# Flamingo-style gated cross-attention with a quantised FFN: projections, y and denominators of two segments in one cluster

## The reference, cut to what matters

```python
def _L0_xattn_ref(latents, context, ...):       # latents: layernorm(x), 2048 x 256; context: 1601 x 256
    lat = layernorm(latents, ln_l_w, ln_l_b)
    ctx = layernorm(context, ln_c_w, ln_c_b)
    q = (lat @ Wq).reshape(b, n, H, D).transpose(0, 2, 1, 3)      # H = 16 heads, D = 64
    k, v = jnp.split(ctx @ Wkv, 2, axis=-1)                       # heads as q
    attn = jnp.einsum('bhnd,bhsd->bhns', q, k) * D ** (-0.5)
    attn = jax.nn.softmax(jnp.clip(attn, -11.0, 11.0), axis=-1)
    out = jnp.einsum('bhns,bhsd->bhnd', attn, v)
    return out.transpose(0, 2, 1, 3).reshape(b, n, INNER) @ Wo + bo
x = x + jnp.tanh(g_xattn[0]) * _L0_xattn_ref(_layernorm(x, axis=-1), ctx_1024, ...)
x = x + jnp.tanh(g_ffn[0]) * _L0_ffn_ref(_layernorm(x, axis=-1), w_gate, w_up, w_down)
```

## Time and profile before

| | before |
|---|---|
| median of 3 runs | 1151.55 us (1150.32 to 1151.62) |
| the profiled execution | 1151.44 us, span 1149.6 us |
| PE busy | 1075.3 us, 94% of the span |
| DVE busy | 1006.2 us, 88% |
| ACT busy | 604.5 us, 53% |
| chain that ended last | PE 80%, DVE 9%, ACT 5%, issue 5% |
| granted TensorE clock, mean | 0.981 |

### The profile page before, as it was taken

One profiled execution on the slowest core, in us unless ns is written; L12 is line 12 of the kernel. 1 busy time (PEld: TensorE's weight loads), 2 busy tenths in 40 slices (PEclk: granted clock), 3 DMA queues, 4 the chain that ended last, 5 costly groups with the idle time before them and its releaser, 6 DMA issues.

```text
span 1149.6 us, 20469 instructions
## 1 busy us (share of the span) xinstructions
PE 1075.3 (94%) x8342; PEld 501.4 (44%) x8342; DVE 1006.2 (88%) x1390; ACT 604.5 (53%) x706; POOL 37.0 (3%) x41
## 2 busy tenths in 40 slices
PE   5999999999999999999999999999999998999059
PEld 3443344434443444344434443444344323887049
DVE  7687988898989898999898989887999999749996
ACT  3555555555555555555555555554555464449652
POOL 0500000000000000000000000000000000003200
PEclk9999999999999999999999999999999999999579
DMA  8001300010001000100010001000000000000002
GB/s 264 18 20 25 120 20 20 20 38 20 20 20 37 20 20 20 38 20 19 21 38 20 20 20 38 20 20 20 30 20 19 20 29 10 1 1 1 0 0 74
DMA packets 37860, 34.57 MB, mean 30 GB/s; under 512 B 14209, under 2 KB 28738, under 8 KB 37510
## 3 DMA queue, kind: packets, MB, share of 16 engines
q1 hardware_dynamic: 37766, 33.26, 9.4%
HBM read 30.75 MB, written 2.36 MB: 29 GB/s over the span
## 4 chain that ended last, share of the span: by engine, by line
PE 80%; DVE 9%; ACT 5%; issue 5%; DMA 0%; POOL 0%; POOLq 0%; SPq 0%; DVEq 0%; ACTq 0%
PE ps L1384 26%; PE ps L1400 26%; PE ps L1247 5%; PE ps L1312 4%; PE ps L1257 4%; PE ps L1265 4%; PE ps L1534 3%; PE ps L1579 3%; DVE acc L925 2%; PE ps L1276 1%; DVE e_buf L1022 1%; DVE gt L1174 1%; ACT z L746 1%; ACT e_buf L664 1%; ACT z L748 1%
## 5 line engine op out<-in xcount | busy, mean ns | idle before, releaser
L664 ACT ACTIVATE e_buf<-ps 128x1024 f32<-128x1024 f32 x400 | 410.4, 1026 | 310.6 <-PE ps L1384 302.3
L1400 PE MATMUL ps<-e_buf,vb 64*64 64x512 f32 x3072 | 401.2, 593 | 4.7 <-DVE e_buf L1022 4.6
L925 DVE TENSOR_TENSOR acc<-acc,e_buf 128x1024 f32<-128x1024 f32 x318 | 387.8, 1220 | 0.0
L1022 DVE TENSOR_SCALAR e_buf<-e_buf 128x1024 f32<-128x1024 f32 x400 | 274.8, 687 | 53.9 <-ACT e_buf L664 52.6
L1384 PE MATMUL ps<-qb,kb_odd 64*64 64x512 f32 x1600 | 208.7, 589 | 0.0
L1384 PE MATMUL ps<-qb,kb_even 64*64 64x512 f32 x1600 | 208.6, 589 | 0.0
L1400 PEld LDWEIGHTS ps<-e_buf,vb 64*64 64x64 f32 x3072 | 111.7, 133 | 221.4 <-issue 187.4
L1384 PEld LDWEIGHTS ps<-qb,kb_odd 64*64 64x64 f32 x1600 | 61.5, 133 | 109.9 <-issue 109.6
L1384 PEld LDWEIGHTS ps<-qb,kb_even 64*64 64x64 f32 x1600 | 61.3, 133 | 110.2 <-issue 110.1
L1011 DVE TENSOR_TENSOR xacc<-ps,xacc 128x512 f32<-128x512 f32 x60 | 41.2, 690 | 35.4 <-PE ps L1312 34.9
L1534 PE MATMUL ps<-hT,wgu 128*128 128x512 f32 x288 | 67.7, 396 | 0.1
(11 more groups left out here) (151 smaller groups left out, 776.9 us busy)
## 6 DMA issues: line engine op xcount, KB each, us to landing
ebc<-el_rows SPq DMA_DIRECT2D x64, 128.0 KB, 2.9
rden<-inv_rows SPq DMA_DIRECT2D x62, 128.0 KB, 2.9
xacc<-in_x_dram SPq DMA_DIRECT2D x4, 512.0 KB, 7.2
wst<-in_L_xattn_Wkv_dram SPq DMA_DIRECT2D x16, 128.0 KB, 2.7
out_dram<-z SPq DMA_DIRECT2D x7, 256.0 KB, 2.5
wst<-in_L_xattn_Wq_dram SPq DMA_DIRECT2D x8, 128.0 KB, 2.7
wo_raw<-in_L_xattn_Wo_dram SPq DMA_DIRECT2D x8, 128.0 KB, 3.4
acc<-in_ctx_dram SPq DMA_DIRECT2D x2, 512.0 KB, 7.5
```

Source lines behind the costliest of these rows:

```text
L664: nc.scalar.activation(e_buf[:, g % E_BUFS, :, :], sc[:, g % 2, :, :], ACT.Exp, scale=float(DH) ** -0.5).then_inc(exp_done, 1)
L925: dve.tensor_tensor(acc[:, t0 % 3, :, :], a, e_buf[:, tiles_to(t0, st) % E_BUFS, :, :], ALU.add).then_inc(summed, 1)
L1022: dve.tensor_scalar(tile, tile, EXP_LO, EXP_HI, ALU.max, ALU.min).then_inc(clip_done, 1)
L1400: ins = pe.matmul(ps_o[DH * h:DH * h + DH, half, :], vb[rows, p % 2, st, DH * h:DH * h + DH], e_buf[rows, g % E_BUFS, h, :], start=(st == ...
```

## The change

Segments 2 to 23 (`BOTH`) are taken two by two. The even one's cluster has the jobs of both: two key/value blocks, the queries of the next two segments, four halves of y (segments t-4 and t-3), and the denominators. The odd one has no jobs, so that its tiles follow the even one's in one run of 25. The scaling of segments t-4 and t-3 (`scaled_in`) stands in the even one too, ahead of their y. There are three query buffers instead of two. DVE does two thirds of weight preparation in an even segment instead of one in each, from segment 6 on, and three weight transposes are due in segments 14, 16 and 18 instead of 14, 15 and 16.

```diff
--- before.py
+++ after.py
@@ -31,14 +31,15 @@
 SB = -(-S // NB)
 LN3 = ST + NT
 SEGS = PAIRS * NBS
-PREP0 = 7
+PREP0 = 6
+BOTH = range(2, SEGS - 2 * NBS)
 PREP = (4, 5, 0, 1, 2, 3)
 ORDER = [(t // NBS, t % NBS) for t in range(SEGS - 2 * NBS)]
 ORDER += [(PAIRS - 2, b) for b in range(NBS - 1)] + [(PAIRS - 1, b) for b in range(NBS - 1)]
 ORDER += [(PAIRS - 2, NBS - 1), (PAIRS - 1, NBS - 1)]
 WT0 = ORDER.index((PAIRS - 1, 0))
 TURNED = (2, 0, 1)
-WT_AT = {14: [(2, 0)], 15: [(2, 1)], 16: [(2, 2)],
+WT_AT = {14: [(2, 0)], 16: [(2, 1)], 18: [(2, 2)],
          WT0: [(0, 0), (0, 1)], WT0 + 1: [(0, 2), (1, 0)], WT0 + 2: [(1, 1), (1, 2)]}
 WT_ORDER = [key for t in sorted(WT_AT) for key in WT_AT[t]]
 ROWS_AT = FULL - 4
@@ -127,11 +128,20 @@
 
 def kv_blocks(t):
 
+    if t in BOTH:
+        return [] if t % 2 else [(t // NBS + 1, t % NBS), (t // NBS + 1, t % NBS + 1)]
     if t < SEGS - 2 * NBS:
         return [(t // NBS + 1, t % NBS)] if t else [(1, 0)]
     return {WT0 - 3: [(PAIRS - 1, 0)], WT0 - 2: [(PAIRS - 1, 1)], WT0 - 1: [(PAIRS - 1, 2), (PAIRS - 1, 3)]}.get(t, [])
 
 
+def q_blocks(t):
+
+    if t in BOTH:
+        return [] if t % 2 else [t + 1, t + 2]
+    return [t + 1] if t + 1 < SEGS else []
+
+
 def turn_of(t):
 
     return next((i for i, segs in enumerate(DENS) if t in segs), None)
@@ -148,12 +158,16 @@
 
 def y_segments(t):
 
+    if t in BOTH:
+        return [t - 4, t - 3] if t % 2 == 0 and t >= 4 else []
     early = [t - 4] if 4 <= t <= WT0 + 2 else []
     return early + ([t - 2] if t > WT0 else [])
 
 
 def scaled_in(t):
 
+    if t in BOTH or t == BOTH.stop:
+        return [t - 4, t - 3] if t % 2 == 0 and t >= 4 else []
     if t == WT0:
         return [t - 3, t - 2]
     return [t - 3] if 3 <= t < WT0 else []
@@ -171,8 +185,7 @@
     jobs = [(0, ("el",))] if t == 2 else []
     for p, b in kv_blocks(t):
         jobs += [(0, ("k", p, b)), (0, ("v", p, b))]
-    if t + 1 < SEGS:
-        jobs += [(0, ("q", t + 1))]
+    jobs += [(0, ("q", s)) for s in q_blocks(t)]
     for s in y_segments(t):
         jobs += [(0, ("y", s, 0)), (0, ("y", s, 1))]
     if turn_in(t) is not None:
@@ -245,7 +258,7 @@
             latT = sb("latT", [P, KT, N], stack=att)
             vb = sb("vb", [P, 2, ST, P], stack=att)
 
-            qb = sb("qb", [P, 2, NB], stack=att)
+            qb = sb("qb", [P, 3, NB], stack=att)
             kb = [sb(name, [P, KEYS], stack=att) for name in ("kb_even", "kb_odd")]
             e_buf = sb("e_buf", [P, E_BUFS, 2, NB], stack=att)
             acc = sb("acc", [P, 3, 2, NB], stack=att)
@@ -566,7 +579,7 @@
             def q_take(seg, t):
                 key = ("q", t)
                 await_job(act, key, seg)
-                nc.scalar.copy(qb[:, t % 2, :], ps_m[:, bank_of(key), :]).then_inc(job_taken[bank_of(key)], 1)
+                nc.scalar.copy(qb[:, t % 3, :], ps_m[:, bank_of(key), :]).then_inc(job_taken[bank_of(key)], 1)
 
             def k_take(seg, p, b):
                 key, w = ("k", p, b), cols_of(b)
@@ -691,8 +704,8 @@
                         for p, b in kv_blocks(t0):
                             k_take(seg, p, b)
                             v_take(seg, p, b)
-                        if t0 + 1 < SEGS:
-                            q_take(seg, t0 + 1)
+                        for s in q_blocks(t0):
+                            q_take(seg, s)
                         if turn_in(t0) is not None:
                             den_take(seg, turn_in(t0))
                         for m, j in WT_AT.get(t0, []):
@@ -1055,15 +1068,18 @@
                     if st == 2:
                         for m, j in WT_AT.get(t0, []):
                             w_low(m, j)
-                    if st == 2 and PREP0 <= t0 < PREP0 + 3 * len(PREP):
-                        n, third = divmod(t0 - PREP0, 3)
-                        if third == 0:
-                            w_scales(n)
-                        elif third == 1:
-                            w_multiply(n, 2, w_inverse, w_scaled)
-                        else:
-                            w_integers(n)
-                            w_multiply(n, 1, w_round, w_quant)
+                    if st == 2 and t0 % 2 == 0 and t0 in BOTH:
+                        for third in range(t0 - PREP0, t0 - PREP0 + 2):
+                            n, part = divmod(third, 3)
+                            if not 0 <= n < len(PREP):
+                                continue
+                            if part == 0:
+                                w_scales(n)
+                            elif part == 1:
+                                w_multiply(n, 2, w_inverse, w_scaled)
+                            else:
+                                w_integers(n)
+                                w_multiply(n, 1, w_round, w_quant)
                     if st == 2 and t0 >= WT0:
                         add_last_key(t0 - 1, 0)
                         if t0 == SEGS - 1:
@@ -1382,7 +1398,7 @@
                     for h in range(2):
                         rows = slice(DH * h, DH * h + DH)
                         ins = pe.matmul(sc[HALF * half:HALF * half + HALF, g % 2, h, :], kb[ORDER[t][0] % 2][rows, key0:key0 + HALF],
-                                        qb[rows, t % 2, :], start=True, stop=True)
+                                        qb[rows, t % 3, :], start=True, stop=True)
                 ins.then_inc(scores_ready, 1)
 
             def values(seg, st):
@@ -1481,7 +1497,7 @@
                         if kind == "den":
                             den_job(seg, DENS[turn_in(t0)])
                         elif kind == "q":
-                            q_job(seg, t0 + 1, loaded(ORDER[t0 + 1][0], seg))
+                            q_job(seg, key[1], loaded(ORDER[key[1]][0], seg))
                         elif kind == "k":
                             k_job(seg, key[1], key[2], loaded(key[1], seg))
                         elif kind == "v":
```

## The result

| | before | with the change |
|---|---|---|
| median | 1151.59 us (4 runs) | 1166.92 us (4 runs, 1166.01 to 1167.51) |
| ratio | 1 | 1.0134, 95% interval 1.0122 to 1.0147 |
| span of the profiled execution | 1149.6 us | 1164.6 us |

The kernel is 15.3 us slower; the forecast was 16.8 slower (1168.2), in a range of 1162.5 to 1173. A second measurement (f0) gave 1166.78 us (4 runs, 1165.91 to 1170.29), 1.0144 (1.0128 to 1.0159) of before.

The account below looks back on a forecast made before the run. PE, 94% busy, was taken as the bound, with DVE as full inside a run of tiles. Terms 16.7 + 3.1 - 3.0 = +16.8 us gave 1168.2 us, range 1162.5 to 1173.

Parts of the forecast that it names:

- eleven stalls: Odd segments 3 to 23, values of tile 0: PE waits for join_out, 1.52 us each with restart, +16.7 us.
- lateness behind segments 14, 16, 18: Two thirds of weight preparation make DVE late; PE waits in segments 15, 17, 19: +3.0 us, plus 0.1 in 14.
- merged clusters: Even clusters: one entry and exit less a pair (11 x 0.16), plus 6 x 0.2 at short key blocks: -3.0 us.
- nothing behind the stall is late: After the odd stall: some 3 us of DVE work, 3.7 with the next clip, before tile 3's values at 5.1 us.
- short pairs: Six pairs with the short last key block: query projection waited for the key's copy; 0.2 us back each.
- DVE enters the run 1.4, 0.8 and 0.8 us late: After clusters 14, 16, 18: room 1.70 us, thirds needing 3.1, 2.5, 2.5; join_out of 15, 17, 19 equally later.
- At no cost: ScalarE's takes, third query buffer, two scalings before y in the same cluster, and SP's queue add no time.
- Rival 1: Long run: DVE late after each stall, its 1.736 us a tile sets the pace; 2.6 us more, 1171; chance 0.12.
- Rival 2: Clock falls after each of eleven stalls, 1.7 us each, 19 us more, 1187; chance 0.04.
- the clock stays at 1.00: Sign that the forecast is right; a granted clock under 1.00 before 950 would instead show the clock falling.
- The drain rule: Tiling-mode changes drain the engine; 22 go; forecast took 0.11 us for the way in; about 0.85 would outweigh stalls.
- Rival 3: Odd segments: join_out done within 0.1 us of PE's last score matmul, no stall, 1148.4 us; chance 0.04.

Follow-up runs that it names:

- f0: The changed kernel unaltered, measured again on the chip of later runs: 1166.78 us, 1.0144 of the kernel before.
- e1: Changed kernel with one query projection given back from each even cluster to the odd segment, the rest still merged: 1151.65 us, 1.0007 of before.
- e2: Changed kernel with PE's scores kept three tiles ahead in odd segments 3 to 23, no job moved: 1157.86 us, 1.0060 of before.
- e3: Changed kernel with ScalarE's bank copy before the shared part and DVE's join_out before the shared tile's add, odd segments 3 to 23: 1159.27 us.
- e4: Changed kernel with weight preparation cut to one third in segments 14, 16 and 18, the rest in 20 to 26: 1163.84 us.
- h1: Changed kernel plus scores three ahead, ScalarE copying both banks, join_out in the next cluster, an earlier DVE add, weight preparation moved: 1148.03 us, 0.9973 of before.
- g2: Changed kernel with only DVE's second shared-tile add cut to 16 of 512 columns in odd segments 3 to 23: 1167.16 us, 1.0132 of before.
- f1: Changed kernel with scores three tiles ahead and the early join_out together: 1158.01 us, 1.0064 of before.
- g1: f1 with DVE's second shared-tile add cut to 16 of 512 columns in odd segments 3 to 23: 1149.83 us, 0.9985 of before.

## Why the prediction was right, point by point

| | forecast | seen |
|---|---|---|
| eleven stalls | +16.7 | +16.6 (11 x 1.51) |
| lateness behind segments 14, 16, 18 | +3.1 | +2.4 |
| merged clusters | -3.0 | -3.6 |
| sum | +16.8 | +15.4 |

The sum is that of the eleven pairs in the two traces. No term was saved by an error of another: all three are off to the same side.

**The mechanism and its place** were right: the wait is for `join_out`, at the values of tile 0, in segments 3 to 23, eleven times. Shown by the trace, by cover given back (e1), by a dose of it (e2), and by moving the waited-for end (e3).

**The size of one stall.** Forecast 1.52 with entry and restart, seen 1.46 to the weight load and 0.05 behind it: 1.51. The distances of the earlier trace rows carried over to the hundredth, because what is queued on DVE and ScalarE up to there was not touched. That nothing behind the stall is late was right too, though its sum was low: `join_out`, clip, add and shared add take 3.9 us (311.56 to 315.43) and not some 3, with the next clip 4.6 (to 316.12) and not 3.7. The clip still ends before the values of tile 3 start, 5.2 us after those of tile 0 (317.50), so the conclusion stands.

**What the merged clusters save.** Forecast 3.0 in all, seen 3.6: with the lateness gone (e4) the eleven pairs take 13.0 us more than before, of 16.6 for the stalls. A merged cluster with full blocks is 15.36 us to the values (273.11 to 288.47). The two clusters of before make 8.22 (269.90 to 278.12) and 7.22 (300.60 to 307.82), 15.44. The difference lies in the projection that opens a cluster: it takes 1.83 us (273.11 to 274.94) where the second one takes 1.72 (276.72 to 278.44). So the way in costs 0.11 ahead of this projection and about 0.1 more inside it, and the forecast took the first alone from the earlier trace rows. The 0.25 that a pair of h1 saves fits this and the exit of 0.05. The short pairs came as forecast, 1.16. The two y halves fell in line as the earlier trace rows said: in the merged cluster their weights load 0.97 and 0.94 apart. 0.2 of the 3.6 is no saving of a merged cluster but a wait that the forecast left out. Before, the values of segment 15 already waited for clips behind its weight transpose: its pair took 58.01 us, and 56.67 for a short pair with 0.58 for each of two transposes is 57.83.

**The lateness of segments 15, 17 and 19** was forecast as 3.0 plus 0.1 and is 2.4 (the three pairs of e4 against the changed kernel), the largest miss in the sum. In the step "DVE enters the run 1.4, 0.8 and 0.8 us late", the two thirds were put at 3.1 us and took 2.87, so DVE was 1.17 late in segment 14. The 1.07 us that this cost is split: about 0.3 inside the even half, where the values wait for clips and fall behind themselves, 0.74 at the next odd segment. The forecast had put nearly all of it at the odd segment.

**"At no cost"** held in the changed kernel: scalings ahead of y in the same cluster, the third query buffer, SP's queue. The projection put back (e1) leaves all of them in place and costs nothing. In e2 and h1, where the stall that lets DVE catch up is shorter or gone, the two scalings of segment 24 do hold up its y.

**Rival 1 (DVE becomes the bound)** did not decide in the changed kernel (g2), where a stall gives DVE time. It is true one step later, when the stall is taken away (f1, g1). My forecast priced it from the 0.02 us a tile alone. It left out that the odd boundary adds `join_out` and one addition more (the shared tile is added twice) to DVE's work, and that DVE had the second cluster for these before.

**Rival 2 (the clock falls)** was right in kind and wrong in number. In the result's own trace the clock stays at 1.00 from 100 to 750 us. In f0's, of the same kernel, it falls behind two of the eleven stalls (to 0.51 behind the first), at 1.7 us each, and in g2's behind one. That is the rival's price, paid for some of the long stalls and not after each of eleven. That none fell in the result's profiled execution is luck, and the forecast's "the clock stays at 1.00" holds for one of the kernel's two traces. By the Trainium skill (TensorE: Matmul & The Clock Gate, Why this matters for your kernels), idle gaps put the engine back to half rate. The traces of f0 and g2 agree with it, at 0.51 behind a stall of 2.20 us. What decides whether a stall of 2.1 to 2.2 us is followed by a fall stays open.

**The drain rule.** By the Trainium skill (TensorEngine Tiling (Array Packing), Key Properties), a change of tiling mode drains the engine. The traces agree that it costs something: one way in less is worth about 0.2 us, twice what the forecast took from the earlier trace rows, and the way out 0.05. At 0.85 a switch the change would have been free, and it was not.

**Rival 3 (no stall)** fell with the first line of the trace.

## What to carry to other kernels

A cluster of unrelated work between two tiles may be what hides a read-out of accumulators that have no second buffer. Before such work is moved away, look for the waits behind it that have ended long before their engine comes to them, and subtract: when the releaser ends, minus when the engine would be free without that work. After one wait is taken off, add up the next engine's work over the whole stretch, too: a saved wait at the start of a run comes back at its end if that engine has no slack.

## What the runs showed that I had not expected

Two remedies of 9.1 and 7.7 us gave 8.8 together (1166.8 to 1158.0). The second was worth nothing on top of the first: it lets DVE idle for 0.51 us at the start of a run that DVE's work bounds. And ScalarE's three accumulator copies fit around two exponentials without delaying PE (h1). A stall of some 2 us can also cost more than itself, as the clock fell behind three of nine.
